# Expert routing in a two-layer perceiver block: a selection over eight picks per token in place of a mask over 32 experts, and two reordered steps around it

## The reference

```
logits = x @ gate_weight.T
probs = softmax(logits)
topv, topi = top_k(probs, 8)
topv = topv / clip(topv.sum(-1), 1e-12)
scaled = topv * layer_alpha
active = scaled >= 0.05
empty = ~any(active);  fallback = arange(8) == argmax(scaled)
active = active | (empty & fallback)
routing_weights = topv * active
routing_weights = routing_weights / clip(routing_weights.sum(-1), 1e-12)
combine = zeros((T, 32)).at[arange(T)[:, None], topi].add(routing_weights)
for each expert: out += (silu(x @ w_g.T) * (x @ w_u.T)) @ w_d.T * combine[:, expert]
```

## Time and profile before

| | us |
|---|---|
| median of 3 runs | 2234.73 (2233.13 to 2237.29) |
| profiled execution, its own time | 2233.13 |
| its span in the trace | 2231.3 |
| PE busy | 2081.5 (93%) |
| DVE busy | 1148.2 (51%) |
| POOL busy | 967.4 (43%) |
| ACT busy | 788.5 (35%) |

### The profile page before, as it was taken

How to read it: one execution, slowest core, us unless ns; L and a number is a source line. 1 busy time by engine, 2 the same in 40 slices (tenths; PEclk the granted TensorE clock), 3 DMA queues, 4 the chain that set the end, 5 groups by cost and what they waited for, 6 DMA issues and landing times. The chain is left out here.

```text
span 2231.3 us, 28141 instructions
## 1 busy us (share of the span) xinstructions
PE 2081.5 (93%) x8874; PEld 1400.0 (63%) x8874; DVE 1148.2 (51%) x2690; ACT 788.5 (35%) x1978; POOL 967.4 (43%) x937
## 2 busy tenths in 40 slices
PE   7997999999888999999998899998986999999995
PEld 5775766677567864566664676657764555555553
DVE  4216777655734112355553777757874343444443
ACT  1124433324431210033333434334543444444551
POOL 1017555321256210076777555637501444555552
PEclk8998999999999999999999999999996999999998
DMA  3231000120021000011113000210034999998886
GB/s 117 79 114 57 22 22 22 35 77 1 21 93 57 32 33 1 0 52 40 53 52 107 23 22 22 75 64 1 1 133 144 294 317 302 239 219 214 212 214 167
DMA packets 84544, 209.21 MB, mean 94 GB/s; under 512 B 13856, under 2 KB 39968, under 8 KB 76928
## 3 DMA queue, kind: packets, MB, share of 16 engines
q1 hardware_dynamic: 61680, 153.54, 20.2%
q0 software_dynamic: 21280, 51.38, 11.3%
q10 hardware_dynamic: 1440, 2.49, 0.3%
HBM read 257.95 MB, written 34.36 MB: 131 GB/s over the span
## 5 line engine op out<-in xcount | busy, mean ns | idle before, releaser
L98 PE MATMUL banks<-L1f_w,L1f_xT 128*128 x760 | 265.1, 492 | 2.5 <-ACT L1f_xT L2339 1.5
L2523 POOL DMA_INDIRECT moe_sums<-L1f_y,L1f_row x95 | 150.6, 1585 | 221.4 <-DVE L1f_is_who L2392 150.6
L159 POOL TENSOR_TENSOR rstd<-rstd,power 128x1 f32<-128x1 f32 x48 | 28.7, 599 | 416.1 <-DVE rstd L153 416.1
L98 PEld LDWEIGHTS banks<-L1f_w,L1f_xT 128*128 128x128 f32 x760 | 138.1, 192 | 82.4 <-issue 7.5
L2531 POOL DMA_INDIRECT L1f_xg<-moe_rows,L1f_row x95 | 94.2, 991 | 65.0 <-DVE L1f_row L2387 38.5
L448 PE MATMUL banks<-L0x_wn,L0x_qT 128*128 128x512 f32 x256 | 115.1, 593 | 0.8 <-DVE x L518 0.8
L448 PE MATMUL banks<-L1x_wn,L1x_qT 128*128 128x512 f32 x256 | 115.1, 593 | 0.8 <-DVE x L518 0.8
L489 ACT ACTIVATE L1x_prob<-banks,L1x_small 128x256 f32<-128x256 f32 x128 | 58.9, 472 | 159.7 <-DVE L1x_small L531 159.7
L489 ACT ACTIVATE L0x_prob<-banks,L0x_small 128x256 f32<-128x256 f32 x128 | 58.9, 472 | 158.7 <-DVE L0x_small L531 158.7
L2359 DVE SCALAR_TENSOR_TENSOR L1f_z<-banks,L1f_share,L1f_sg 128x192 f32<-128x192 f32 x95 | 39.7, 418 | 145.9 <-ACT L1f_sg L2294 145.8
L98 PE MATMUL banks<-L0f_down,L0f_z 128*128 128x512 f32 x256 | 111.1, 593 | 1.5 <-DVE L0f_z L1852 1.5
(11 more groups left out here) (395 smaller groups left out, 5257.2 us busy)
## 6 DMA issues: line engine op xcount, KB each, us to landing
L1f_w<-in_experts SPq DMA_DIRECT2D x95, 1280.0 KB
L1f_laid<-moe_counts SPq DMA_DIRECT2D x59, 512.0 KB, 5.5
w<-in_L1x_heads SPq DMA_DIRECT2D x16, 704.0 KB, 4.0
w<-in_L0x_heads SPq DMA_DIRECT2D x16, 608.0 KB, 3.8
w<-in_wug SPq DMA_DIRECT2D x8, 1024.0 KB, 4.7
L0x_craw<-in_ctx SPq DMA_DIRECT2D x96, 64.0 KB, 2.0
L1x_craw<-in_ctx SPq DMA_DIRECT2D x96, 64.0 KB, 2.0
w<-in_L0x_out SPq DMA_DIRECT2D x4, 1280.0 KB, 5.6
```

Source lines behind the costliest of these rows:

```text
L98: ins = pe.e.matmul(out, w, m, start=first and n == 0, stop=last and n == len(pairs) - 1)
L2523: pool.e.indirect_dma_start(self.sums[j % 2][:, :], bass.IndirectOffsetOnAxis(ap=self.row[:, j:j + 1], axis=0), self.y[j % self.NY][:], No ...
```

## The change

`choose` no longer makes `rest`. `fall_back` becomes `weigh`: it works out the final weight of each of the eight picks on 32 columns (four tiles by eight picks). `combine_tiles` no longer works on four tiles of 32 columns at once. For each tile it compares the expert numbers with the eight picks (128x256: eight picks by 32 experts), multiplies by the eight weights, and sums over the picks; the sum reads its input with the picks innermost, so that neighbouring elements of a sum lie 32 words apart. On PE, `count(0)` now stands ahead of `ask(7)`, and on ACT `exponents(1)` stands behind the copy of the first half of `upto`.

```diff
@@ turns of the tiles, PE
         self.turn_tile(pe, NT - 1)
         self.begin(pe)
+        self.count(pe, 0)
         self.ask(pe, NT - 1)
-        self.count(pe, 0)
         self.count(pe, 1)
@@ scalar
-        self.exponents(act, 1)
         act.wait_ge(self.counted, 1)
         act.e.copy(self.upto[:, 0:BANK], sh.psum(3)).then_inc(self.upto_set.sem, 1)
+        self.exponents(act, 1)
@@ choose
-            self.then(dve, e.match_replace(self.rest[:, a + i, :], top[:, i, :], pb[:, i, :], -1.0))
@@ fall_back -> weigh
-        self.then(dve, e.tensor_tensor(scaled, top, self.per_tile(one[:, 3, :], TOPK), ALU.mult))
-        self.then(dve, e.tensor_scalar(scaled, scaled, self.alpha[:, 0:1], None, ALU.mult))
+        self.then(dve, e.tensor_tensor(rw, top, self.per_tile(one[:, 3, :], TOPK), ALU.mult))
+        self.then(dve, e.tensor_scalar(scaled, rw, self.alpha[:, 0:1], None, ALU.mult))
+        self.then(dve, e.tensor_scalar(active, scaled, TAU, None, ALU.is_ge))
...
         self.then(dve, e.tensor_tensor(fb, same[:, :, 1:], same[:, :, 0:TOPK], ALU.is_gt))
-        self.then(dve, e.scalar_tensor_tensor(out=fb, in0=atf, scalar=1.0, in1=fb, op0=ALU.add, op1=ALU.mult))
-        self.then(dve, e.tensor_reduce(one[:, 6, :], fb, AX_X, ALU.add))
-        self.then(dve, e.tensor_tensor(one[:, 6, :], one[:, 6, :], one[:, 5, :], ALU.mult))
+        self.then(dve, e.tensor_tensor(fb, fb, self.per_tile(one[:, 5, :], TOPK), ALU.mult))
+        self.then(dve, e.tensor_tensor(active, active, fb, ALU.max))
+        self.then(dve, e.tensor_tensor(rw, rw, active, ALU.mult))
+        self.then(dve, e.tensor_reduce(one[:, 6, :], rw, AX_X, ALU.add))
+        self.then(dve, e.tensor_scalar(one[:, 6, :], one[:, 6, :], 1e-12, None, ALU.max))
+        self.then(dve, e.reciprocal(one[:, 6, :], one[:, 6, :]))
+        self.then(dve, e.tensor_tensor(rw, rw, self.per_tile(one[:, 6, :], TOPK), ALU.mult))
@@ combine_tiles (the ten steps on 128 columns of four tiles go)
-        self.then(dve, e.tensor_tensor(part, pb, self.per_tile(one[:, 3, :], NE), ALU.mult))
...
-        self.then(dve, e.tensor_tensor(combine, part, self.per_tile(one[:, 7, :], NE), ALU.mult), self.combined)
-        e.tensor_scalar(self.member[:, a:b, 0:NE], combine, 0.0, None, ALU.is_gt).then_inc(self.members.sem, 1)
+        experts = self.iota[:].rearrange("p (o n) -> p o n", o=1).to_broadcast([P, TOPK, NE])
+        for i in range(a, b):
+            at, weight = (t[:, i, :].rearrange("p (k o) -> p k o", o=1).to_broadcast([P, TOPK, NE]) for t in (self.atf, self.rw))
+            pick = self.pick[i % 2]
+            self.then(dve, e.tensor_tensor(pick[:], experts, at, ALU.is_equal))
+            self.then(dve, e.tensor_tensor(pick[:], pick[:], weight, ALU.mult))
+            self.then(dve, e.tensor_reduce(self.combine[:, i, :], pick[:].rearrange("p k n -> p n k"), AX_X, ALU.add),
+                      self.combined if i == b - 1 else self.routing)
+        e.tensor_scalar(self.member[:, a:b, 0:NE], self.combine[:, a:b, :], 0.0, None, ALU.is_gt).then_inc(self.members.sem, 1)
```

More of the change, by code:

```diff
@@ L1966, in __init__ @@
         self.combine, self.pb = sb("combine", [P, NT, NE]), sb("pb", [P, NT, NE])
-        self.rest, self.part, self.only = (sb(n, [P, NT, NE]) for n in ("rest", "part", "only"))
-        self.top, self.atf, self.scaled, self.fb = (sb(n, [P, NT, TOPK]) for n in ("top", "atf", "scaled", "fb"))
+        self.pick = [sb(f"pick{i}", [P, TOPK, NE]) for i in range(2)]
+        self.top, self.atf, self.rw, self.scaled, self.active, self.fb = (
+            sb(n, [P, NT, TOPK]) for n in ("top", "atf", "rw", "scaled", "active", "fb"))
         self.same = sb("same", [P, NT, TOPK + 1])
@@ L2137, in rows_early @@
         if i == 12:
-            self.fall_back(dve, 0)
+            self.weigh(dve, 0)
     def turn_early(self, pe, i):
@@ L2347, in vector @@
         self.choose(dve, 1)
-        self.fall_back(dve, 1)
+        self.weigh(dve, 1)
         self.combine_tiles(dve, 1)
@@ L2462, in choose, with weigh @@
             self.then(dve, e.max_index(self.at[:, a + i, :], top[:, i, :], pb[:, i, :]))
-            self.then(dve, e.match_replace(self.rest[:, a + i, :], top[:, i, :], pb[:, i, :], -1.0))
-    def fall_back(self, dve, g):
+    def weigh(self, dve, g):
         (a, b), e = self.GROUPS[g], dve.e
-        one, top, atf, scaled, fb, same = (t[:, :, a:b] if t is self.one else t[:, a:b, :] for t in (
-            self.one, self.top, self.atf, self.scaled, self.fb, self.same))
+        one, top, rw, scaled, active, fb, same = (t[:, :, a:b] if t is self.one else t[:, a:b, :] for t in (
+            self.one, self.top, self.rw, self.scaled, self.active, self.fb, self.same))
         ends = scaled.rearrange("p i k -> p k i")
-        self.then(dve, e.tensor_copy(atf, self.at[:, a:b, :]))
+        self.then(dve, e.tensor_copy(self.atf[:, a:b, :], self.at[:, a:b, :]))
         self.then(dve, e.tensor_reduce(one[:, 3, :], top, AX_X, ALU.add))
@@ L2488, in combine_tiles @@
+        self.then(dve, e.tensor_tensor(rw, rw, active, ALU.mult))
[3 more added lines that the diff above has]
+        self.then(dve, e.tensor_tensor(rw, rw, self.per_tile(one[:, 6, :], TOPK), ALU.mult))
     def combine_tiles(self, dve, g):
         (a, b), e = self.GROUPS[g], dve.e
-        n, one = b - a, self.one[:, :, a:b]
@@ L2492, in combine_tiles @@
-        pb, rest, part, only, combine = (t[:, a:b, :] for t in (self.pb, self.rest, self.part, self.only, self.combine))
-        experts = self.iota[:].rearrange("p (o n) -> p o n", o=1).to_broadcast([P, n, NE])
-        self.then(dve, e.tensor_tensor(part, pb, self.per_tile(one[:, 3, :], NE), ALU.mult))
-        self.then(dve, e.scalar_tensor_tensor(out=part, in0=rest, scalar=0.0, in1=part, op0=ALU.is_lt, op1=ALU.mult))
-        self.then(dve, e.scalar_tensor_tensor(out=only, in0=experts, scalar=1.0, in1=self.per_tile(one[:, 6, :], NE),
-                                              op0=ALU.add, op1=ALU.is_equal))
```

## The result

The changed kernel takes 2246.66 us as the median of 6 runs (2244.63 to 2248.88), the kernel before beside it 2234.35 (6 runs, 2233.13 to 2237.29). The ratio is 1.0053, with a 95% interval of 1.004 to 1.0066: slower by 12.3 us, with 9 to 15 us as the ends. That is half a per cent, and clear of the scatter.

What follows compares the result with a forecast made beforehand. PE paces the blocks, so delays ahead of them, mostly on DVE, delay the end: +8.59 us to `choose(1)` and +3.36 in group 1 make +11.95, say +12.0, median 2246.7 us, range 2242 to 2251.

Steps and rivals of the forecast that it cites:

- PE's exchange: Ahead of `choose(1)`: `count(0)` and `ask(7)` wait for `member` and run with DVE idle, 5.00 us no longer hidden.
- The reduction: Sum over picks in `combine_tiles` on DVE: 0.66 us per tile, with 0.42 and 0.89 as the ends.
- `weigh`: DVE, replacing `fall_back`: 3.99 us, +1.13 in group 1; in group 0 all covered by PE except 0.23.
- `choose`: DVE, group 1: one MATCH_REPLACE fewer per tile, four in a group, -1.17 us.
- `combine_tiles`: DVE: four tiles take 6.42 us where ten steps took 3.02, +3.40 us for a group.
- ACT's exchange: Copy ahead of `exponents(1)` on ACT: costs nothing while PE is in `ask(7)`; without that cover, its 0.6 us.
- The free read: Rival on the DVE reduction: the stepped read costs nothing extra; sum +10.1 us, median 2244.8; chance 24%.
- The steep read: Rival on the DVE reduction: the 32-word step costs twice L503's excess; sum +13.8 us, median 2248.5; chance 12%.
- The clock did not move against the change: Rival on PE's first blocks: upper clock comes one block later, +3 us, about 2250, or one earlier, about 2244; chance 9%.
- The clock that stays up: Rival on PE from `count(0)` through the first block: clock at 2.4 GHz, leaving about +2 us, 2236.9; chance 3%.

Runs made afterwards that it cites:

- e2_swap_only: Kernel before the change with only the two reorderings, on PE and on ACT, made; median 2240.72 us against 2234.66, ratio 1.0023.
- e8_no_act_swap: Changed kernel with only ACT's reordering undone, PE's new order kept; median 2246.37 us, ratio 1.0051 to the kernel before.
- e7_act_swap_only: Kernel before the change with only ACT's two steps reordered, PE's order as it was; median 2236.05 us against 2234.50, ratio 1.0006.
- e3_picks_inner: Changed kernel with `pick` laid as 32 experts by 8 picks, so the sum reads neighbouring words; 2245.11 us, ratio 1.0049 to the kernel before.
- the ninth kernel: Kernel before the change with only seven unread matmuls added on PE between `count(0)` and `count(1)`, none in the plan; 2232.78 us, ratio 0.9988.

## Why the prediction held, term by term

The direction, the place and the size held: 2246.7 us was forecast, 2246.66 measured. The agreement to less than 0.1 us is luck. The sum was 12.0 us and the trace has 11.2; the runs' median rose by 12.3, in an interval of 9 to 15.

- **PE's exchange.** The burst `count(0)`, `ask(7)` is in the open as forecast, with DVE idle for 4.95 us. From `member` to `choose(1)` are 5.18 us, where the working had 0.28 + 3.22 + 1.78 + 0.03 = 5.31: the two matmul rows (3.22 from 1689.33, 1.75 from 1692.35) overlap by 0.20 us, and `member` to `count(0)` took 0.37. `e2_swap_only` shows that the exchange does this by itself.
- **The reduction.** Taken at 0.66 us, measured at 0.585: eight of them make -0.6, most of the 0.8 between sum and trace. It was the one term without a row of its own kind. The nearest row, L503's stepped write, gave too much, yet lay closer than either end (0.42 and 0.89). The estimate from the section on measured stream behaviour in the Trainium skill's "Vector Engine (DVE) Microarchitecture Reference" (1.73 ns per column for one source that hops 4 KiB at every element, where here it steps 32 words) was 0.60 us, and the measured 0.585 agrees with it better than my own.
- **`weigh`.** 3.97 us were measured for 3.99, +1.11 in group 1, and +0.20 for 0.23 in group 0, where PE's work covers the rest: L1479 no longer waits (0.95 us idle in the earlier trace rows, none now).
- **`choose`.** 4.01 us from 1694.14 to 1698.15, where before it took 5.18: -1.17, as forecast.
- **`combine_tiles`.** 6.13 us in place of 3.02, +3.11 for the +3.40 of the text; the difference is the reduction's.
- **ACT's exchange.** Free, as forecast (`e8_no_act_swap`). But the remark that without cover it would cost the copy's 0.6 us was wrong: `e7_act_swap_only` shows 3.1 us in the trace, 2.99 of them one wait. What is queued ahead of the exponential is not only the copy but also the copy's wait for `count(0)`. A moved step brings its wait with it.
- **The rivals.** The free read (+10.1) falls with the 0.585 of the rows and with `e3_picks_inner`, which has it at 0.42 only with neighbouring words. The steep read (+13.8) falls likewise. The clock did not move against the change: the gap ahead of `count(1)` grew to 14.44 us, as feared, and the first block took 5.19 us where it took 5.48. The clock that stays up did not come: PE's granted clock in the changed kernel is 0.50 from 1684 until the first block, and `ask(7)` took 1.75 us. Its arithmetic held something real all the same. The experiments with unread matmuls reach the upper clock, and that is worth 6.0 us in the traces and 5.5 in the medians, less than the 7.5 that the rival put on these pieces. It had them halve, and only the first block comes near that (5.48 to 2.84 us); the plan's pieces go to about 0.6 of their time (`count(1)` 1.43 to 0.85, the limits 1.22 to 0.73). Whether the changed kernel would gain as much is not shown: every kernel with unread matmuls was built from the kernel before.

What stays open: the source of the 3.04 us ahead of the common start. The distance between the two traces is 2.5 us at the first L1479 (518.8 and 521.3), 5.4 at the last L1852 of layer 0's feed-forward part (816.6 and 822.0) and 3.1 at the first L1570 of layer 1's self attention (1574.2 and 1577.3), so it comes and goes in code that is the same in both, and over all traces the start moves between 1668.82 and 1675.11 us. No run isolates what moves it.

## What to carry to other kernels

An instruction that is moved ahead of another takes its wait along: `count(0)` ahead of `ask(7)` put `member`, and 5 us of PE work that DVE had covered, between the last logits and the routine that reads them. On a chain of dependent small steps count the steps times their width: fewer columns in the weights' arithmetic did not pay once the picks were spread over 256 columns for each tile. And where PE paces the end, look at its granted clock just before: here matmuls that nobody reads, put into PE's waits, gave 5.5 us in the medians, more than the one reordering that won anything (`member` early, 1.6 us).

## What the runs showed of the hardware

- A DVE reduction of 128x256 f32 that reads words 32 apart takes 0.58 to 0.59 us, with neighbouring words 0.42: 0.6 ns more for each element. The stepped write of L503 costs more, 0.91.
- Operands that repeat one number cost nothing extra, whichever of the two sources repeats along the innermost direction: L2499 and L2500 take 0.42 to 0.43 us in both layouts, as L1877 does, which repeats nothing (0.420).
- PE at 1.2 GHz runs the four passes of `count(1)` in 1.43 us and a block's first eight in 5.5 at most, at 2.4 GHz in 0.85 and 2.84. Before, with PE busy for 10.27 of 18.50 us, the lower level stayed through the whole plan; with 13.46 of 14.00 us busy the upper one did. In the ninth kernel it rose in the gap and fell again in the plan (granted 1.00 up to 1700, then 0.51).
- The first block's eight matmuls vary with where the clock returns: 5.48 us before, where it was granted 0.50 for the whole of them (to 1718.3), 5.19 after, where it came back in their last half microsecond, 4.28 in `e3_picks_inner`, where it was up for about the last 1.4 us. Up to 1.2 us of a difference between two traces can come from there alone.
